# Ones by ScalarE for two rounds instead of three, unit 0's first step among the picks, eight empty products, and first-layer steps from unit 6

## The reference

```python
e = jnp.stack([tbl_0[ids[:, 0]], ..., tbl_39[ids[:, 39]]], axis=1)   # 512 x 40 x 32
iidx, jidx = jnp.triu_indices(40, k=1)
z = jnp.einsum('bpd,pde,bpe->bp', e[:, iidx, :], bilinear_matrices, e[:, jidx, :])
h = jnp.concatenate([z, dense_ctx], axis=1)                          # 512 x 796
h = jnp.maximum(h @ W_top1 + b_top1, 0.0)                            # 512
h = jnp.maximum(h @ W_top2 + b_top2, 0.0)                            # 256
y = h @ W_top3
```

## Time and profile before

| | us |
|---|---|
| median of three runs | 196.93 (195.64 to 197.13) |
| the profiled execution | 195.53 |
| its span, first to last instruction | 193.7 |
| PE, DVE, POOL, ACT busy | 181.1, 146.1, 116.0, 48.0 |
| mean granted clock of TensorE | 0.974 of full |
| first issues of SyncE's queue: ids, hot ids, hot table | 0.74, 1.19, 1.65 |

### The profile page before, as it was taken

How to read it: one execution, slowest core, us unless ns; L and a number is a source line. 1 busy time by engine, 2 the same in 40 slices (tenths; PEclk the granted TensorE clock), 3 DMA queues, 4 the chain that set the end, 5 groups by cost and what they waited for, 6 DMA issues and landing times.

```text
span 193.7 us, 3692 instructions
## 1 busy us (share of the span) xinstructions
PE 181.1 (93%) x1550; PEld 54.2 (28%) x1550; DVE 146.1 (75%) x145; ACT 48.0 (25%) x60; POOL 116.0 (60%) x119
## 2 busy tenths in 40 slices
PE   6998597899399999999999999999999999999994
PEld 2343243322022223232232232323223223222320
DVE  1899595494547999888988989989889889886500
ACT  2499995201011111011211112001211111110313
POOL 3777887777777777777777777899922220220000
PEclk9999999966969999999999999999999999999999
DMA  5999855699501273100100372000004600000000
GB/s 157 383 412 402 333 153 162 177 335 283 122 14 15 61 210 96 15 14 14 14 17 14 88 211 68 14 3 3 2 0 124 176 28 0 5 0 0 3 0 0
DMA packets 12441, 20.00 MB, mean 103 GB/s; under 512 B 3700, under 2 KB 6648, under 8 KB 12296
## 3 DMA queue, kind: packets, MB, share of 16 engines
q1 hardware_dynamic: 8888, 18.10, 28.3%
q0 software_dynamic: 3072, 1.58, 4.8%
q10 hardware_dynamic: 464, 0.09, 0.3%
HBM read 11.89 MB, written 0.00 MB: 61 GB/s over the span
## 4 chain that ended last, share of the span: by engine, by line
PE 77%; ACT 9%; DMA 5%; issue 3%; DVE 3%; SPq 1%; ACTq 1%; DVEq 0%
PE y_ps L534 33%; PE z_ps L550 25%; PE t_ps L463 10%; PE y_ps L463 6%; DMA table<-hot_tables 4%; ACT z_t L357 3%; ACT plane L347 3%; DVE prod L446 3%; PE t_ps L483 2%; DMA z_t<-dense 2%; ACT z_t L359 1%; PE z_ps L483 1%; ACT xt L366 1%; ACT xt L367 1%; ACTq L398 1%
## 5 line engine op out<-in xcount | busy, mean ns | idle before, releaser
L446 DVE TENSOR_TENSOR prod<-y_ps,xt 128x1024 f32<-128x1024 f32 x100 | 116.0, 1218 | 25.1 <-PE y_ps L534 24.9
L276 POOL DMA_INDIRECT x_rows<-rows,row x96 | 92.9, 968 | 29.2 <-issue 28.9
L534 PE MATMUL y_ps<-xt,m_sb 32*128 32x512 f32 x400 | 71.0, 664 | 0.6 <-DVE prod L446 0.5
L550 PE MATMUL z_ps<-prod,sel 128*32 128x512 f32 x400 | 54.9, 624 | 0.4 <-DVE prod L446 0.4
L534 PEld LDWEIGHTS y_ps<-xt,m_sb 32*128 32x128 f32 x400 | 23.6, 189 | 47.6 <-issue 30.4
L422 DVE TENSOR_SCALAR hot<-hot_id,number 128x2048 bf16<-128x2048 int16 x33 | 22.5, 748 | 8.3 <-DMA hot_id<-hot_ids 4.2
L463 PE MATMUL t_ps<-z_t,table 128*32 128x512 f32 x176 | 23.0, 593 | 3.1 <-DMA z_t<-dense 3.1
L284 POOL TENSOR_TENSOR hot_id<-x_rows,hot_id 128x512 f32<-128x512 f32 x6 | 7.7, 1275 | 25.1 <-ACT x_rows L391 25.1
L550 PEld LDWEIGHTS z_ps<-prod,sel 128*32 128x32 f32 x400 | 8.1, 110 | 40.5 <-issue 21.8
L483 PE MATMUL y_ps<-hot,plane 128*32 128x512 bf16 x192 | 14.6, 380 | 0.5 <-ACT plane L347 0.5
L391 ACT ACTIVATE hot<-t_ps 128x512 f32<-128x512 f32 x8 | 4.8, 597 | 34.1 <-PE t_ps L463 34.1
(11 more groups left out here) (39 smaller groups left out, 67.3 us busy)
## 6 DMA issues: line engine op xcount, KB each, us to landing
xt<-xt SPq DMA_DIRECT2D x20, 192.0 KB, 2.5
xt<-xt SPq DMA_DIRECT2D x20, 128.0 KB, 2.5
hot_id<-hot_ids SPq DMA_DIRECT2D x4, 512.0 KB, 7.1
table<-w SPq DMA_DIRECT2D x1, 1792.0 KB, 8.4
x_rows<-rows,row POOLq DMA_INDIRECT x96, 2.4
table<-hot_tables SPq DMA_DIRECT2D x2, 640.0 KB, 8.9
xt<-xt SPq DMA_DIRECT2D x20, 64.0 KB, 2.7
table<-hot_tables SPq DMA_DIRECT2D x2, 512.0 KB, 5.3
```

The costliest lines, as they stand in the source:

```text
L276: pool.indirect_dma_start(out=x_rows[:, g, c, :], out_offset=None, in_=rows, in_offset=bass.IndirectOffsetOnAxis(ap=row[:, n:n + 1], axis= ...
L446: nc.vector.tensor_tensor(prod[:, k % PROD_UNITS, 2 * half:2 * half + 2, :], y_ps[:, 2 * slot:2 * slot + 2, :], partners[half], ALU.mult). ...
L534: last = nc.tensor.matmul(y_ps[:, 2 * slot + place % 2, :], m_sb[rows, k, :], xt[rows, u, :], start=True, stop=True)
L550: last = nc.tensor.matmul(z_ps[s * DIM:(s + 1) * DIM, :], window, prod[:, k % PROD_UNITS, place, :], start=first, stop=(k == last_unit(b)) ...
```

## The change

Four things, and one transfer. (1) ScalarE makes ones for rounds 14 and 33 in place of 14, 21 and 30, and those of 33 come after the planes of the last position; VectorE makes the other 34. (2) The first step of unit 0 is moved out of the schedule and stands before round 33 of the picks; the code of a unit's first step becomes a function. (3) After unit 1 and after unit 2 TensorE runs four products of 128 columns by 512 each on old ones, into `t_ps`, whose result nobody reads; before the first of them it waits for all four hot positions to be rebuilt (`x_out`). (4) First-layer steps 0 and 1 stand after units 6 and 7 instead of 4 and 6. The ids are issued first on ScalarE's queue instead of SyncE's.

```diff
@@ -73,8 +73,11 @@
 HOT_RING = 6
 UPPER_LEAD = 2
 
-BY_SCALAR = {14: 0, 21: 1, 30: 2}
-ONES_RING = 3
+BY_SCALAR = {14: 0, 33: 1}
+ONES_RING = 2
+
+EARLY_ROUND = 33
+FILL_AFTER = {1: 4, 2: 4}
 PIECE_RING = 2
 HOT_BANK = [(0, 1), (2, 3), (4, 5), (6, 7)]
 
@@ -96,7 +99,7 @@
 
 
 AFTER = {
-    "l1": [4, 6, 8, 10, 12, 14, 16, 18, 20, 22, 24, 26, 28, 30, 32, 34, 36, 38, 40, 42, 45, 47],
+    "l1": [6, 7, 8, 10, 12, 14, 16, 18, 20, 22, 24, 26, 28, 30, 32, 34, 36, 38, 40, 42, 45, 47],
     "turn": [0, 8, 18, 24, 32, 38],
 }
 
@@ -296,7 +299,6 @@
                 cols = slice(0, HOT_ROWS[o] * DIM)
                 sp.dma_start(table[:, o, :, cols], hot_tables[:, o, :, cols]).then_inc(table_in[o], 16)
 
-            sp.dma_start(ids_sb[:], ids).then_inc(ids_in, 16)
             load_hot_ids(0)
             load_tables(0)
             load_hot_ids(1)
@@ -330,6 +332,7 @@
 
         @block.scalar
         def _(act):
+            act.dma_start(ids_sb[:], ids).then_inc(ids_in, 16)
             act.dma_start(number[:], numbers).then_inc(number_in, 16)
             act.dma_start(negative[:], negatives).then_inc(negative_in, 16)
             act.dma_start(sel[:], select).then_inc(sel_in, 16)
@@ -371,10 +374,9 @@
             make_ones(scalar_rounds[0])
             rebuild(0)
             make_planes(2)
-            make_ones(scalar_rounds[1])
             rebuild(1)
             make_planes(3)
-            make_ones(scalar_rounds[2])
+            make_ones(scalar_rounds[1])
             rebuild(2)
             rebuild(3)
             for what, k in steps:
@@ -471,6 +473,35 @@
                     by_columns(y_ps[:, LATE_BANK[m], :], w1_sb[:, LATE_BLOCK, m * P:(m + 1) * P], z_t[:, LATE_BLOCK, :],
                                True, False)
 
+            def first_steps(k):
+
+                nonlocal chunks_seen
+                t, u = UNIT[k]
+                if MAT0[chunks_seen] <= k:
+                    pe.wait_ge(mats_in[chunks_seen], 16)
+                    chunks_seen += 1
+                if all(w != u for _, w in UNIT[:k]):
+                    x_there(pe, u)
+                for s in range(G):
+                    half = 2 * k + s // 2
+                    slot = half % Y_SLOTS
+                    place = INNER_PLACE[s] if t == u else s
+                    if s % 2 == 0 and half >= Y_SLOTS:
+
+                        pe.wait_ge(prod_done, half - Y_SLOTS + 1)
+                    elif s % 2 == 0:
+                        pe.wait_ge(x_out, 2 * half + 2)
+                    rows = slice(s * DIM, (s + 1) * DIM)
+                    last = nc.tensor.matmul(y_ps[:, 2 * slot + place % 2, :], m_sb[rows, k, :], xt[rows, u, :],
+                                            start=True, stop=True)
+                    if s % 2 == 1:
+                        last.then_inc(y_done, 1)
+
+            def fill(n):
+
+                for _ in range(n):
+                    nc.tensor.matmul(t_ps[:], hot[:, 0, 1, 0:P], hot[:, 0, 0, :], start=True, stop=True)
+
             pe.wait_ge(cleared, 1)
             zeros = prod[:, 0, 0, :].bitcast(BF16)
             for _ in range(WARM):
@@ -485,6 +516,8 @@
                 return done
 
             for j in range(len(ROUND) + UPPER_LEAD):
+                if j == EARLY_ROUND:
+                    first_steps(0)
                 if j < len(ROUND):
                     o, r = ROUND[j]
                     if j in BY_SCALAR:
@@ -515,26 +548,12 @@
                     pe.wait_ge(z_out, b + 1)
                     by_columns(t_ps[:], w1_sb[:, b, m * P:(m + 1) * P], z_t[:, b, :], True, True).then_inc(part_done, 1)
                 if what == "unit":
...
+                    if k > 0:
+                        first_steps(k)
+                    if k in FILL_AFTER:
+                        if k == min(FILL_AFTER):
+                            pe.wait_ge(x_out, 2 * HOTS)
+                        fill(FILL_AFTER[k])
                 if what == "sum":
                     b, r = place_of(k)
                     first = r == 0
```

## The result

| | before | changed |
|---|---|---|
| median of the runs, us | 196.28 (195.61 to 197.13) | 185.58 (185.34 to 186.19) |
| the profiled execution, us | 195.53 | 185.34 |
| its span, us | 193.7 | 183.5 |
| mean granted clock | 0.974 | 0.999 |

What follows compares the result with a forecast made beforehand. TensorE bounds the steady state. Unit 1 starts at 32.3 us, then 15.2 to unit 7 and 12.2 to unit 11 at 59.7, 12.1 earlier: 183.4, plus 0.9 for the median, 184.3 us (8 in 10: 181.5 to 188.5).

Steps and rivals of the forecast that it cites:

- Start of the queues: Ids off SyncE's queue: its loads issued about 0.45 us earlier; gain between 0 and 0.45, taken as 0.45.
- Rounds 21 and 30: In the picks: PE's waits of 2.2 and 1.6 us for ScalarE's ones go, as VectorE makes both at 0.67 a round.
- Unit 0 early: Before round 33: the same 1.14 us of PE, moved; VectorE's two products run behind the picks, 29.5 to 31.9.
- Fills: Eight empty products after units 1 and 2: 1.7 us (range 1.7 to 3.1) plus a wait, 2.1 in all, holding the clock.
- Dense rows: Before the first-layer step at 46.6: they land 5.0 us after block 0's copy starts, at 44.8, so no wait is left.
- Units 7 to 10: Now with three first-layer steps: 10.9 us bare plus 1.3 of waits, 12.2, so unit 11 starts at 59.7.
- The low clock before: In the kernel before, between unit 0 and unit 7: the low clock accounts for 5.0 us of the 10.8 beyond bare costs.
- The falling clock: Rival: the clock falls all the same, half of a low stretch, 1.7 to 3.5 us, 186 to 188; chance 0.22.
- Waits for copies: Rival: VectorE waits for copies or gathers longer than given, 3 us more, about 187; chance 0.12.
- Starved picks: Rival: VectorE cannot feed the picks with ones and the 3.8 us stay, 188; chance 0.05.
- a long low clock: Rival: the clock falls after the fills and stays low through the units; 28 us or more give 198 or more; chance 0.03.

## Why the prediction was right, and where its terms were off

The direction, the size and the range held; the 12.1 us were 10.2. The sum is better than its parts. Added alone, the ones bring 4.9 us, and taken back alone, the two steps cost 5.9, which is all of the 10.7; unit 0 early and the empty products, at a cost of 2.1 us to hold the clock, gained nothing that can be measured. The forecast had 3.8 us for the ones, 3.1 for the dense wait and 5.0 for the clock. That these sum to nearly the measured time is in part luck.

*Start of the queues.* Forecast 0.45 earlier, measured none: round 19 starts at 19.68 against 19.69. The number table took 5.15 us to land, more than the 4.5 of its neighbour, so VectorE started 0.8 late and PE waited 1.0 us in all for its ones in the early rounds. The step that failed is that ScalarE's planes set the pace; with VectorE late, the wait for planes vanished behind it. "DMA: Bandwidth & Descriptors" of the Trainium skill, section "Issuing engines are not separate DMA queues", says that transfers of all issuers interleave on the same engines and that another issuer saves only issue time. The trace agrees with it: the hot ids leave at 0.74 and not at 1.19, and that is all. The low end that the prediction drew from it was the better guide: the gain was 0. The ids, first on ScalarE's queue, took 4.7 us to land, where they took 2.0 at the head of SyncE's. With the number table ahead of them 0.3 us of the 0.45 came.

*Rounds 21 and 30.* 3.8 us forecast; from round 19 to round 32 it was 12.2 us before (19.69 to 31.90) and is 8.4 now (19.68 to 28.10). VectorE's 0.67 us a round sufficed.

*Unit 0 early.* The mechanism stated is there (VectorE's products run behind the picks), but the price was forgotten: the 1.2 us by which it delays the weights' issue. With the steps from unit 6 it gained nothing; left out, unit 11 starts 0.9 us earlier. With the steps from unit 7 no pair of runs differs in it alone.

*Fills.* 0.97 to 1.04 us a group of four where 0.85 was taken, and 0.4 us of wait as forecast. The upper bound came from the warm-up products "at the low clock"; the profile of before grants 1.00 from 1.5 to 7 us, so no row shows that they ran low. That the fills keep the clock up was not shown; units 1 to 6 stayed at 1.00 without them.

*Dense rows.* The term that was mis-sized. The prediction moved their landing with block 0's copy, 5.0 us, to 44.8. It was 49.12, 8.6 us after the copy, and TensorE stood 1.8 us. That the landing moves with the copy was not wrong (without the empty products it did, by 1.1 us); the 5.0 us were, for before the four were issued as the queues were about to empty (the DMA share is 0.53 from 50 to 51 us), and now while they are full. The same stretch of the prediction had the number needed, 14.9 us of full DMA engines after the weights' issue, and used it for the copies (47.3, and VectorE's product of unit 6 did start at 47.23), but not for the four small transfers in the same crowd. Unit 7 started at 50.43 and not 47.5: 0.6 from the start and picks, 1.8 from this wait, the rest from fills, halves and a step 0 of 1.06 us for 0.86.

*Units 7 to 10.* 11.2 us, not 12.2: VectorE had caught up during TensorE's wait, so only 0.3 of the 1.3 us of waits came.

*The low clock before.* The account charged it with 5.0 us. The runs of the kernel before that came with the experiments speak against this: 195.55 at a clock of 0.982 and 195.57 at 0.965 in one job. That gap in the clock is 6.6 us more at half speed and would be 3.3 us of time. In the 25 executions of the three groups those at 0.964 to 0.965 are in the mean 0.6 and 0.7 us slower than those at 0.980 to 0.982 on two chips, and 0.4 faster on the third. So a good part of the low time before cost next to nothing. Which part is not shown, since one execution alone is traced. A wait behind it, such as that for the dense rows, can hide it, but only as far as the landing does not move with TensorE, and in part it does. By the marks the 10.2 us read like this: step 0 starts 3.5 us earlier (52.88 to 49.37), since the weights leave 2.6 earlier and the dense rows take 0.9 less after them; and 6.7 less from there to unit 11, since units 5 and 6 and sums 3 and 4 (4.1 bare) are done ahead of the wait, about 1.7 for the clock behind it, and 0.9 of waits for halves. The last two are what remains of the sum; no run takes them apart.

*The rivals.* The falling clock came, in two of six executions of one job and in none of the four of the first, where the prediction had 0.22. What it said for this rival, no idle gap over 0.5 us before the first fall, holds only from 31 us on: the waits of 2.0 and 1.4 us that end at 23.2 and 30.6 come before it too. In the kernel with the ones alone these are gone, and the clock fell all the same. Waits for copies came at 0.7 us, inside the forecast. Starved picks and a long low clock did not.

## What to carry to other kernels

Ask for each wait on a small transfer what is in the queues when it is issued. Its time to landing in one kernel holds for another only if the queues are as full there; issued into a load of megabytes, it waits for much of it. Then put independent work before the wait: here step 0 two units later and step 1 one unit later were worth 5.9 us, and both one unit later again brought about 2. Before work is moved ahead of a point, look at what is released at that point: here a microsecond of unit 0 among the picks delayed 3.8 MB of loads (1792 and 512 KB of weights, two sets of copies of 768 KB). Time lost ahead of a wait was lost only in part here, so it can't be counted in full as a gain; how much depends on whether the awaited thing moves along, and that takes a run.

## What the hardware showed that was not expected

Four transfers of 8 KB issued into the crowd took 5.8 to 6.6 us from the last issue to landing in seven traces; issued at its end, 2.7 to 3.2. The 20 KB number table took 2.2 to 2.3 us in the first place of ScalarE's queue when 96 KB of ids headed SyncE's, 4.4 in the same place when 512 KB of hot ids did, and 5.1 in the second: what the other queue sends at that moment counted for more than the place.

After an idle stretch of 2.0 us of TensorE the clock fell to 1.2 GHz in the traced execution, and it seems so in one other of six of the same kernel, while it stayed at 2.4 in four. In the kernel with the steps from unit 4 it fell 3.8 us into an idle stretch of 5.8, and was low for 6.8 us. But after 2.8 us idle in the kernel with the ones alone it stayed at 2.4, and after 3.1 in the kernel before it fell. "TensorE: Matmul & The Clock Gate" of the Trainium skill, section "HAM oscillation — how this bites in real kernels", blames idle gaps. The falls after 2.0, 3.1 and 5.8 us fit that, though not every such gap brought one; the fall at 36.5 us in the kernel with the ones alone, with no idle gap over 0.6 us ahead of it from 7 us on, does not.
